# A graph network with routed experts on one core: when side transfers are issued in layer 1, and how the last expert blocks and the last wait are ordered

## The reference

```python
# _L0_gnn_ref, on layernorm(x); self loops are appended to the edges
deg = segment_sum(ones, dst); dis = rsqrt(deg); norm = dis[src] * dis[dst]
for l in range(2):
    h = x @ W[l]
    agg = segment_sum(norm[:, None] * h[src], dst) + b[l]
    x = relu(agg + x_res @ resW + resb)
# _L0_ffn_ref, on layernorm(x)
rh = relu(features @ router_w1 + router_b1)
top_w, top_i = top_k(softmax(rh @ router_w2 + router_b2), 2)
gates = softmax(top_w)
out = sum over the 2 chosen experts: gate * (relu(relu(f @ w1 + b1) @ w2 + b2) @ w3 + b3)
```

## Time and profile before

| | |
|---|---|
| median of 3 runs | 1825.99 us (1825.48 to 1828.19) |
| the profiled execution | 1823.8 us, span 1822.2 us |
| TensorE busy | 1761.7 us (97%) |
| DVE, ACT, POOL busy | 1028.1, 801.3, 305.8 us |
| granted TensorE clock, mean | 0.994 of full speed |
| sum matmuls, line 1488 | 4704, 1072.1 us |
| DMA | 293.95 MB, mean 161 GB/s |

### The profile page before, as it was taken

How to read it: one execution, slowest core, us unless ns; L and a number is a source line. 1 busy time by engine, 2 the same in 40 slices (tenths; PEclk the granted TensorE clock), 3 DMA queues, 4 the chain that set the end, 5 groups by cost and what they waited for, 6 DMA issues and landing times. The chain is left out here.

```text
span 1822.2 us, 40926 instructions
## 1 busy us (share of the span) xinstructions
PE 1761.7 (97%) x14272; PEld 1039.3 (57%) x14272; DVE 1028.1 (56%) x2775; ACT 801.3 (44%) x1719; POOL 305.8 (17%) x339
## 2 busy tenths in 40 slices
PE   6988899999999999999999999999999998999997
PEld 5764444445444544454444444444444487888886
DVE  8686565656566565656234444444444568555554
ACT  5876455555555555555312222222222232656663
POOL 1654100000000000000001111111111133333333
PEclk9999999999999999999999999999999999999999
DMA  8414952333333332424665555555555488224442
GB/s 263 122 23 162 215 190 112 153 128 137 135 131 149 114 158 105 166 97 169 244 233 183 185 187 184 184 190 187 184 188 196 164 280 299 81 80 119 139 140 76
DMA packets 106129, 293.95 MB, mean 161 GB/s; under 512 B 13589, under 2 KB 81515, under 8 KB 99784
## 3 DMA queue, kind: packets, MB, share of 16 engines
q1 hardware_dynamic: 90376, 255.13, 39.9%
q0 software_dynamic: 15536, 37.80, 6.6%
q10 hardware_dynamic: 144, 0.13, 0.0%
HBM read 162.27 MB, written 139.22 MB: 165 GB/s over the span
## 5 line engine op out<-in xcount | busy, mean ns | idle before, releaser
L1488 PE MATMUL bank<-parts,counts 128*128 128x512 f16 x4704 | 1072.1, 380 | 5.0 <-DVE counts L1643 5.0
L1488 PEld LDWEIGHTS bank<-parts,counts 128*128 128x128 f16 x4704 | 445.4, 98 | 508.2 <-issue 17.1
L1693 ACT ACTIVATE counts<-bank 128x490 f16<-128x490 f32 (+1 forms) x624 | 318.0, 577 | 326.1 <-PE bank L1590 326.1
L649 DVE TENSOR_TENSOR rows<-rows,iota_lo 128x2560 bf16<-128x2560 bf16 (+1 forms) x336 | 320.7, 996 | 24.8 <-PE bank L1590 21.5
L477 POOL DMA_INDIRECT first_rows<-route_rows,route_spot_i x49 | 47.9, 977 | 1158.1 <-DVE tokens L468 1150.2
L1590 PEld LDWEIGHTS bank<-rows 64*128 64x128 bf16 x6144 | 92.5, 94 | 84.4 <-issue 77.5
L2322 PE MATMUL bank<-y_t,counts 128*128 128x256 f32 x480 | 115.4, 384 | 3.6 <-ACT y_t L2394 3.6
L1590 PE MATMUL bank<-rows 64*128 64x49 bf16 x6144 | 111.0, 184 | 5.1 <-DVE counts L1643 5.1
L1503 ACT ACTIVATE middle<-bank 128x256 f32<-128x256 f32 x98 | 37.9, 387 | 175.4 <-PE bank L1488 161.3
L2322 PE MATMUL bank<-h_t,counts 128*128 128x256 f32 x480 | 114.4, 381 | 0.0
L2351 PE MATMUL bank<-counts,h_t 128*128 128x256 f32 x480 | 113.5, 380 | 0.0
(11 more groups left out here) (279 smaller groups left out, 1716.4 us busy)
## 6 DMA issues: line engine op xcount, KB each, us to landing
counts_table<-counts SPq DMA_DIRECT2D x25, 3136.0 KB, 9.2
counts<-counts_table SPq DMA_DIRECT2D x24, 3136.0 KB, 12.3
res_tile<-res_table SPq DMA_DIRECT2D x98, 128.0 KB, 2.1
counts<-expert_pack SPq DMA_DIRECT2D x31, 257.0 KB, 4.7
rows<-first_rows SPq DMA_DIRECT2D x30, 260.0 KB, 3.8
rows<-second_rows SPq DMA_DIRECT2D x30, 258.0 KB, 2.8
rows<-first_out SPq DMA_DIRECT2D x30, 256.0 KB, 3.8
res_table<-parts SPq DMA_DIRECT2D x7, 896.0 KB, 4.1
```

What stands on the lines that cost most here:

```text
L649: return nc.vector.tensor_tensor(rows, k, v, ALU.is_equal)
L1488: mm = nc.tensor.matmul(acc[:, 0:2 * dim], counts[:, b, s, o * P:(o + 1) * P], parts[:, s, :], start=s == 0, stop=s == tiles - 1)
L1693: nc.scalar.activation(counts[:, b, :, group_nodes(g, o)], group_bank(g, o, b)[:, 0:group_size(g) * tiles].rearrange("p (n s) -> p s n", s ...
```

## The change

Six edits:

1. POOL waits until `sums_ready` of layer 1 is 4 before it issues the zero rows, and until 8, 12, ... 28 before the transfers of expert 0, 1, ... 5.
2. `final_list` is cut into `final_rows` (six operations, step 10) and `final_ends` (eight, step 11).
3. In SP's `loads` the transfer into `held` stands right behind the wait for `result_ready`, ahead of the rows; in step 11 also ahead of the wait for the list.
4. In the last round TensorE does the outputs of block 58 ahead of the second layer of block 59, and DVE adds them ahead of taking that layer's high half.
5. Block 59's outputs go to two banks; each half signals for itself, DVE adds and signals each half, and POOL scatters each half on its own signal.
6. POOL's last wait for the scatters is moved out of the section, behind the branch's end.

```diff
+        PACK_AFTER = 8
+
+        def pack_experts(pool, sums_ready=None):
+
             for e in range(experts):
+                if sums_ready is not None:
+                    pool.wait_ge(sums_ready, PACK_AFTER + 4 * e)
                 for n, w in enumerate((expert_w1, expert_w2, expert_w3)):
...
             def gpsimd(pool):
+                pool.wait_ge(update.sums_ready, PACK_AFTER - 4)
                 store_fillers(pool)
-                pack_experts(pool)
+                pack_experts(pool, update.sums_ready)
...
                     if b == 10:
-                        work.final_list(dve)
+                        work.final_rows(dve)
+                    if b == 11:
+                        work.final_ends(dve)
...
                             else:
                                 sp.wait_ge(result_ready, b + 1)
+                            if isinstance(b, int) and b < 2 * experts:
+                                self.hold(sp, b)
                             if isinstance(b, int) and b + SB == EARLY_BLOCKS:
                                 sp.wait_ge(list_ready, 2)
                                 router.wait_scattered(sp, pairs)
...
-                            if isinstance(b, int) and b < 2 * experts:
-                                self.hold(sp, b)
...
                     for h, cols_of in half:
                         for kf in range(K2):
-                            mm = nc.tensor.matmul(outs_bank[k % 2][:, cols_of], h2_t[:, k % 2, kf, h * P:(h + 1) * P],
+                            mm = nc.tensor.matmul(self.outs_of(k, h, each_half)[:, cols_of], h2_t[:, k % 2, kf, h * P:(h + 1) * P],
                                                   weights_of(k, 2)[:, kf, :], start=kf == 0, stop=kf == K2 - 1)
+                        if each_half and h == 0:
+                            mm.then_inc(outs_ready, 1)
                     mm.then_inc(outs_ready, 1)
+
+                def outs_of(self, k, h, each_half):
+                    return turn_bank if each_half and h == 1 else outs_bank[k % 2]
...
+                            outs_first = last and k == SB - 2
+                            if outs_first:
+                                self.outs(pe, b, k, r)
                             if not (last and k + 1 >= SB):
                                 self.second_layer(pe, b + 1, *ahead(r, k, 1))
                             if isinstance(b, int) and b < 2 * SB:
                                 beside(b)
-                            self.outs(pe, b, k, r)
+                            if not outs_first:
+                                self.outs(pe, b, k, r, each_half=last and k == SB - 1)
...
-                    rounds(pool, NB, BLOCKS, lambda b, k: self.scatter(pool, b, k, out))
+                    rounds(pool, NB, BLOCKS - SB, lambda b, k: self.scatter(pool, b, k, out))
+                    for k in range(SB - 1):
+                        self.scatter(pool, BLOCKS - SB + k, k, out)
+                    self.last_scatter(pool)
+
+                def last_scatter(self, pool):
+
+                    for h, cols_of in half:
+                        pool.wait_ge(result_ready, BLOCKS + h)
...
+                def wait_results(self, pool):
                     for o in range(2):
                         pool.wait_ge(result_stored[o], 32 * NB)
...
                 free_own_sems()
+        work.wait_results(nc.gpsimd)
```

More of the change, by code:

```diff
@@ L2510, in blocks_held, with final_rows @@
                     link(nc.vector.tensor_scalar(more_held[:, :, lean:experts], placed_to[:, :, lean:experts], -1.0, None, ALU.mult))
[L2512 to L2513 removed]
+                def final_rows(self, dve):
+                    link = self.link
                     numbers = block_of[:, :, :].rearrange("p c n -> p (c n)")
@@ L2544, in add_bias, with add_outs @@
                     ins.then_inc(bias_added, 1)
-                def add_outs(self, dve, b, k, c):
+                def add_outs(self, dve, b, k, c, each_half=False):
                     dve.wait_ge(bias_added, b + 1)
-                    dve.wait_ge(outs_ready, b + 1)
                     for h, cols_of in half:
-                        ins = nc.vector.scalar_tensor_tensor(result[:, k % 2, cols_of], outs_bank[k % 2][:, cols_of],
+                        if h == 0 or each_half:
+                            dve.wait_ge(outs_ready, b + (1 + h))
+                        ins = nc.vector.scalar_tensor_tensor(result[:, k % 2, cols_of], self.outs_of(k, h, each_half)[:, cols_of],
                                                              rows[:, k % SB, h, gate_at[c]:gate_at[c] + 1], acc[:, k % 2, cols_of], ALU.mult, ALU.add)
+                        if each_half and h == 0:
+                            ins.then_inc(result_ready, 1)
                     ins.then_inc(result_ready, 1)
@@ L2599, in steps @@
                                     self.normal(dve, b + 4, k + 4, r + (k + 4) // SB)
-                            if not (last and k + 1 >= SB):
+                            outs_first = last and k == SB - 2
+                            if not (last and k + 1 >= SB) and not outs_first:
                                 second(b + 1, (k + 1) % SB)
@@ L2606, in steps @@
                                 dve.wait_ge(result_stored[k % 2], r * (16 * SB) + 32 * (k // 2))
-                            self.add_outs(dve, b, k, c)
+                            self.add_outs(dve, b, k, c, each_half=last and k == SB - 1)
+                            if outs_first:
+                                second(b + 1, (k + 1) % SB)
                     first(1, 1)
@@ L2635, in moves @@
                     rounds(pool, 3 * SB, NB, lambda b, k: self.scatter(pool, b, k, first_out))
-                    rounds(pool, NB, BLOCKS, lambda b, k: self.scatter(pool, b, k, out))
+                    rounds(pool, NB, BLOCKS - SB, lambda b, k: self.scatter(pool, b, k, out))
[5 more added lines that the diff above has]
+                        pool.wait_ge(result_ready, BLOCKS + h)
+                        if h == 0:
+                            pool.sem_inc(passed, 1)
+                        pool.indirect_dma_start(out, bass.IndirectOffsetOnAxis(ap=to_row[:, SB - 1, h:h + 1], axis=0), result[:, 1, cols_of], None,
+                                                bounds_check=out.shape[0] - 1, oob_is_err=False).then_inc(result_stored[1], 16)
+                def wait_results(self, pool):
                     for o in range(2):
```

5 lines of the change are left out of this document (3 added, 2 removed).

## The result

The changed kernel takes 1812.03 us (median of 3 runs, 1811.94 to 1815.18) against 1825.99; the ratio is 0.9926, with a 95% interval of 0.9904 to 0.9949. Forecast were 1815.6 us, so it is 14.0 us faster where 10.4 were expected. Run again with five rounds it took 1812.19 against 1826.72: 0.992 (0.9907 to 0.9934).

The account below looks back on a forecast made before the run. TensorE, busy 97% of the span, bounds the kernel; only its stands, slow clock and the end can shrink. 6.6 + 2.3 + 0.4 + 1.1 = 10.4 us off 1823.8 gives 1813.4, as median 1815.6; range 1811.5 to 1820.

Parts of the forecast that it names:

- B: Expert blocks: TensorE's clock holds after the held-weights wait, step 5.62 not 8.57 us, total 1812.6; chance 0.13.
- part 1: Layer 1: spreading POOL's transfers removes TensorE's 5.09 us stand and 1.52 us of slow clock; gain 6.6 us.
- the landing of the held transfer: Expert blocks: the last held weights, first in their queue, land faster by 0.6 us, bounds 0 to 1.2.
- part 5: Span end: POOL reaches the barrier when the last scatter's issue ends, not at its landing; gain 1.1 us, other bound 0.
- The budget of 19.8 us: Layer 1: time from a result store's issue to DVE's need; spread transfers would keep stores inside it, at no cost.
- Rivals A: Layer 1: the zero rows stall it again, costing up to 6.6 us, total 1822.2; chance 0.06.
- D: Layer 1: experts' batches stall it six times, up to 6.6 us each, 1855 instead of 1815.6; chance 0.04.
- Part 2: Expert blocks: list in two steps removes nearly all of TensorE's 2.68 us in step 10, worth nothing by itself.
- Part 3: Expert blocks: held weights ahead of the rows end the wait for them earlier; gain 2.3 us, bounds 1.1 to 2.9.
- rival C: Expert blocks: held weights land when they did, landing hanging on traffic, not issue; gain 0, total 1817.9; chance 0.10.
- Part 4: Last blocks: reordered outputs and half-by-half signals bring the last scatter's issue to 1814.9 from 1815.32; gain 0.4 us, bounds 0 to 0.9.
- last matmul to span end shorter by 1.5 us: Span end: sign that the forecast is right, the stretch after TensorE's last matmul shrinking by 1.5 us.

Follow-up runs that it names:

- one batch: Changed kernel with the zero rows and all six experts' batches issued together once tile 3 is summed: 1820.15 us, 0.9966.
- both edits: Changed kernel with every held transfer two steps earlier and the list undivided in step 10: 1811.64 us, 0.9912.
- two steps earlier: Changed kernel with every held transfer issued two steps earlier, three of them in step 0: 1808.64 us, 0.9902.
- part 5 alone: Kernel before with one edit, POOL's last wait moved behind the branch: 1822.09 us, 0.9978.
- part 1 or part 5 alone: Kernel before with only POOL's transfers spread over layer 1: 1816.27 us; or with only its last wait behind the branch: 1822.09 us.
- part 4 undone: Changed kernel with the last two blocks' outputs, additions and scatters ordered as before: 1813.98 us, 0.9926.

## Why the prediction was right, and where it was off

*Direction and range were right.* No rival took over, though half of one came true (B, below). Three terms were too small: part 1, the landing of the held transfer, and part 5.

*Part 1, right in its mechanism, small in size.* The budget of 19.8 us decided: stores at 28.2 us stall (one batch), the spread ones don't; the first four counts stores landed in 9.7 to 11.8 us and all of them within 13.5, against 24.1 before. The result stores' landings stand in one profile with the transfers spread (held transfers behind the rows): 5.6 to 14.6 us in the stage of the batches, inside the 19.8 and inside the 15 forecast. The 6.6 us are what the profiled execution had. The runs show 8.5 and 9.8 us in the time, since the stall itself varies (6.6 to 9.7 us in three profiles). Rivals A and D are out: no DMA is waited for in layer 1.

*Part 2, wrong in "worth nothing by itself".* I saw that TensorE's stand would only move to the next wait, and missed that the stand also moves the signals on which SP issues: it pushed block 10's result late, so that two rounds of transfers came 3.2 us apart. Undivided, the segment at full clock is 2.1 us longer, by one trace; the time doesn't show it.

*Part 3, the issue right, the landing wrongly credited.* The transfer was issued 0.02 us after its signal (forecast: within 0.3), worth 0.96 us. The faster landing, 1.6 us, is part 2's. So rival C is out as to its price: the earlier issue did gain. Its premise, that the landing hangs on the traffic, came true in part 2's place. ACT went on 3.4 us earlier relative to the steps, 1543.53 against 1549.46 less the 2.52 us that the blocks' start was earlier (1530.00 against 1532.52), where 2.3 were forecast (bounds 1.1 to 2.9).

*The clock, rival B.* I had the stand unchanged at 3.7 us and the slow step at 8.57 with it. The stand became 2.2 to 2.8 us in eight profiles, seven with parts 2 and 3 and the one with the list undivided, and there the step took 5.69 us three times and 7.22 to 7.38 five times; at stands of 3.2 to 3.9 us it took 7.19 to 8.57, four times of four. So against 8.57 the shorter stand gave back 1.2 to 2.9 us, by execution. The reading "such a stand dropped nothing", of the 2.68 us in step 10, held in four profiles with the list whole and failed in the fifth (both edits, list whole and two steps earlier).

*Part 4, right:* 0.5 us for 0.4, and DVE's last addition waits as forecast.

*Part 5, the step failed.* "POOL goes to the barrier when the issue ends" was the mistake, and with it the price of 1.1 us, issue against landing. The chain of waits of the changed kernel (start, length, what) ends so; L2800 is where the section closes, L2825 the branch:

```profile
1806.64 0.02 POOLq L2800
1806.66 0.06 issue
1806.72 0.04 POOLq L2825
1806.76 0.74 issue
1807.50 0.97 POOL out_dram L2673
```

POOL's sequencer passes both some 0.8 us before the last scatter even starts. What the other engines do there stands in the view of the branch's source line. For POOL, ACT, SP and DVE it is a row of about 0.05 us; TensorE's queue (PEldq) is on it for over 4 us. Changed kernel, then before (times in ns, then the start):

```profile
L2825 PEldq COMPARE_BRANCH  x1: 4142/4142/4142, 1806.8 to 1806.8; - x1
```

```profile
L2785 PEldq COMPARE_BRANCH  x1: 4242/4242/4242, 1817.9 to 1817.9; - x1
```

This row is 4.1 to 4.5 us long in all fourteen profiles, and in thirteen the span ends with it. Before, it starts when the scatter has landed at 1817.4 and the engines have met, 2.6 us after the last issue at 1815.32. In the changed kernel it starts at 1806.84, 0.7 us ahead of the last issue at 1807.50, and runs beside issue and landing. That is the 3.3 us, and it comes out so in both directions: 2.6 us behind the issue with the last wait put back inside, 0.5 us ahead of it with part 5 alone. Why this branch takes TensorE's queue 4.1 to 4.5 us no row shows.

*The sum.* By the runs: 8.5 to 9.8 (part 1), 3.3 (parts 2 and 3 at full clock, 23.69 less 20.36, where before's segment is 26.57 less its slow step's 2.88 over 5.69), 0 to 2.9 of clock (0, since the slow step took as little as 7.19 us in a kernel with the old stand), 0.5, 3.3: 15.6 to 19.8 us, against 16.0 between the median spans (1824.8 and 1808.8). The time fell 14.5 there, because something comes back around the span: 1.4 to 2.6 us in every run of the kernel before, in the eight runs of the changed kernel 2.0 or 2.1 four times and 3.7 to 4.2 four times. With part 1 or part 5 alone all runs have 1.4 to 2.1; with four or all of the five parts every kernel has some runs over 3. It costs 0.9 us on the mean, and which parts bring it stays open. That the time fell inside the range is in part luck: 1812.03 lies 0.5 us above its lower end, and 15.6 us from 1825.99 would have been 1810.4, below it. The sign "last matmul to span end shorter by 1.5 us" came out at 4.8 to 5.0 us: 3.3 of part 5, 0.5 of part 4, and the rest is no gain, since the last matmul now ends 2.4 us before the last issue and not 4.0 (4.0 again with part 4 undone).

## What to carry to other kernels

Price a background transfer by the tightest store behind which an engine waits, and split it until each piece, on top of that store, fits. When a stand is removed ahead of another wait, ask which signals it had delayed and what was issued on them, before calling it worthless; and take a transfer that is only awaited once off the last step altogether (two steps earlier took 2.7 us more off the segment, nearly as much as the 3.3 of parts 2 and 3 together). A wait for the last store belongs behind everything that can run beside its landing, and what the sequencer can pass, it passes before the engine is done. For the end of a span, look at the sequencers' rows of every engine too, by the line of the closing branch; the engine's busy rows and the chain don't show them all.

## What the runs showed that I had not expected

The same stand doesn't always cost the same: after 2.2 to 2.8 us idle TensorE's next step was slow in five profiles and at full clock in three. The last scatter lands 2.1 us after its issue where POOL waits for it inside the section (three kernels), and 3.3 to 3.8 us where the wait stands behind the branch and TensorE's branch row runs beside it (ten kernels). The preparation, in which nothing was changed, ends anywhere between 160.75 and 164.19 us, which is more than parts 2, 3 or 4 are worth; one profile of each kernel can tell the sum wrongly by 3 to 4 us.
